# The rotated convolution of images 0 to 2 on 32x32 tiles of the array

## The reference

```python
x = x + L0(gn(x))   # deformable convolution: 36 points a pixel, 4 corners each, then two dense layers
x = x + L1(gn(x))   # rotated convolution, the layer that is changed
x = x + L2(gn(x))   # linear attention
x = x + L3(gn(x))   # three quantised depthwise-like convolutions
```

## Time and profile before

| | |
|---|---|
| Time, median of 3 runs (lowest, highest) | 8428.0 us (8407.72, 8446.78) |
| Profiled execution: its own time, its span | 8406.53 us, 8404.7 us |
| Mean granted clock of TensorE | 0.711 of full speed |
| Busy: TensorE, its weight loads | 3952.7 us (47%), 2022.5 us (24%) |
| Busy: VectorE | 5151.7 us (61%) |
| Busy: GpSimd (the gathers' instructions) | 4440.0 us (53%) |
| Busy: ScalarE | 1232.6 us (15%) |

### The profile page before, as it was taken

How to read it: one execution, slowest core, us unless ns; L and a number is a source line. 1 busy time by engine, 2 the same in 40 slices (tenths; PEclk the granted TensorE clock), 3 DMA queues, 4 the chain that set the end, 5 groups by cost and what they waited for, 6 DMA issues and landing times.

```text
span 8404.7 us, 44163 instructions
## 1 busy us (share of the span) xinstructions
PE 3952.7 (47%) x11246; PEld 2022.5 (24%) x11246; DVE 5151.7 (61%) x4233; ACT 1232.6 (15%) x1846; POOL 4440.0 (53%) x4684
## 2 busy tenths in 40 slices
PE   6133241341365535442555435442565544428797
PEld 3121121221122213221222113221222222213453
DVE  6667668576566646664666646654666665553556
ACT  1000100001111001111111001111110011112246
POOL 2666656666565655565665655565666555650000
PEclk8566665675687657766787667766787777669899
DMA  4442533534333322244333322244333223441128
GB/s 130 129 128 87 158 113 123 151 109 136 111 107 96 99 85 87 90 153 161 115 96 102 99 81 91 88 159 150 116 113 95 76 89 96 151 149 42 43 99 236
DMA packets 511085, 953.74 MB, mean 113 GB/s; under 512 B 252032, under 2 KB 300928, under 8 KB 494848
## 3 DMA queue, kind: packets, MB, share of 16 engines
q0 software_dynamic: 221184, 604.27, 23.3%
q1 hardware_dynamic: 289792, 348.19, 12.9%
HBM read 791.89 MB, written 160.24 MB: 113 GB/s over the span
## 4 chain that ended last, share of the span: by engine, by line
issue 30%; another core or an unknown queue 26%; DVE 17%; PE 17%; ACT 4%; POOL 3%; DMA 2%; DVEq 1%; SPq 1%; ACTq 0%; POOLq 0%
PE PS L859 16%; DVE ring L1700 6%; DVE dbuf L1706 3%; ACT img L1310 3%; POOL ring L482 3%; DVE PS L1882 1%; DMA img<-d_dram 1%; DVE cb L1767 1%; DVEq L384 1%; DVE img L2067 1%; ACT cb L1310 0%; DVE stats L1762 0%; DVE img L2183 0%; PE PS L1176 0%
## 5 line engine op out<-in xcount | busy, mean ns | idle before, releaser
L482 POOL DMA_INDIRECT ring<-table,idx_stage x4608 | 4422.2, 960 | 3021.7 <-DVE dbuf L1706 1550.4
L1706 DVE TENSOR_REDUCE dbuf<-ring 128x64 f32<-128x2304 f32 x512 | 2071.1, 4045 | 109.6 <-issue 79.8
L859 PE MATMUL PS<-img,wb_sb 128*128 128x512 f32 (+1 forms) x3264 | 1646.0, 665 | 989.4 <-issue 401.9
L1700 DVE TENSOR_TENSOR ring<-ring,PS 128x2304 f32<-128x2304 f32 x480 | 1222.6, 2547 | 119.6 <-DMA ring<-table,idx_stage 101.4
L859 PE MATMUL PS<-img,wa_sb 128*128 (+2 forms) x2908 | 944.3, 635 | 624.2 <-issue 459.7
L859 PEld LDWEIGHTS PS<-img,wb_sb 128*128 128x128 f32 x3264 | 688.3, 215 | 1913.2 <-issue 1692.9
L859 PEld LDWEIGHTS PS<-img,wa_sb 128*128 128x128 f32 (+2 forms) x2908 | 385.2, 166 | 1153.7 <-issue 1123.1
L859 PE MATMUL PS<-wb_sb,img 128*128 128x512 f32 x512 | 344.1, 837 | 518.3 <-ACT cb L1310 221.5
L859 PE MATMUL PS<-wa_sb,cb 128*128 128x256 f32 (+1 forms) x992 | 262.2, 427 | 542.4 <-issue 269.8
L2067 DVE SCALAR_TENSOR_TENSOR img<-PS,params,img 128x512 f32<-128x512 f32 x256 | 179.9, 744 | 507.2 <-ACT img L1310 358.9
L2230 DVE TENSOR_REDUCE sm<-PS 128x16 f32<-128x1024 f32 x64 | 78.3, 1224 | 610.3 <-remote 465.1
(11 more groups left out here) (253 smaller groups left out, 3305.4 us busy)
## 6 DMA issues: line engine op xcount, KB each, us to landing
ring<-table,idx_stage POOLq DMA_INDIRECT x4608
table<-cb SPq DMA_DIRECT2D x64, 512.0 KB
img<-y_dram SPq DMA_DIRECT2D x64, 512.0 KB
q_dram<-img SPq DMA_DIRECT2D x32, 1024.0 KB
img<-q_dram SPq DMA_DIRECT2D x28, 1024.0 KB
img<-in_x SPq DMA_DIRECT2D x8, 2048.0 KB
y_dram<-cb SPq DMA_DIRECT2D x64, 256.0 KB
img<-in_x SPq DMA_DIRECT2D x32, 512.0 KB
```

Of the source, the lines that this page charges most:

```text
L482: nc.gpsimd.indirect_dma_start(out=ring[:, g, p * CORNERS * GC:(p + 1) * CORNERS * GC], out_offset=None, in_=tab[b], in_offset=bass.Indire ...
L859: return nc.tensor.matmul(o, l, r, start=start, stop=stop, **kw)
L1700: last = vec.tensor_tensor(rg, rg, weights.unsqueeze(2).to_broadcast([P, n, GC]), ALU.mult)
L1706: vec.tensor_reduce(dbuf[:, j, g * GC:(g + 1) * GC], ring[:, g, :].rearrange("p (k c) -> p c k", c=GC), AX_X, ALU.add).then_inc(sem("ring_ ...
```

## The change

Images 0 to 2 now go through `l1_packed` too. They can't have bank 7, so they use banks 0 to 3 (`l1_bank`), and each group of four chunks waits until the group before it has been added. On VectorE a turn of the stage is one (quad, k): half of the turn's units, the wait, eleven additions, four statistics, the other half of the units. `lt` has one layout, copied in one instruction, and isn't cleared.

```diff
-        def packed(n):
-            return START + (B - 1) * CHUNKS + n
+        def packed(b, n):
+            return START + b * PAIRS + n
+        def l1_bank(b, j, k):
+            return 2 * j + k if b == B - 1 else j
@@ TensorE, L1
-                def l1(i):
-                    for h in range(2):
-                        n, c = i * 2 + (b * CHUNKS + h), i * 2 + h
-                        room(pe, "lX", n)
-                        for k in range(KC):
-                            for tap in range(K2):
-                                at = R_SIZE + (k * K2 + tap) * P
-                                last = mm(PS[:, 2 * h + k, :].rearrange("p (r x) -> p r x", x=W), wseg(wa_sb, at, P),
-                                          padded(k, c, tap // 3, tap % 3), tap == 0, tap == K2 - 1)
-                        last.then_inc(sem("lC"), 1)
                 def l1_packed(quad, k):
-                    if quad:
-                        pe.wait_ge(sem("lX"), packed(k + 1))
+                    if b < B - 1:
+                        pe.wait_ge(sem("lX"), packed(b, quad * KC + k))
+                    elif quad:
+                        pe.wait_ge(sem("lX"), packed(b, k + 1))
                     for tap in range(K2):
                         for j in range(4):
                             for r in range(4):
                                 ...
-                                last = mm(rows(PS[os_, 2 * j + k, :]), wa_sb[rs, at:at + CG],
+                                last = mm(rows(PS[os_, l1_bank(b, j, k), :]), wa_sb[rs, at:at + CG],
                                           padded(k, quad * 4 + j, tap // 3, tap % 3)[rs], tap == 0, tap == K2 - 1,
                                           tile_position=(r * CG, to * CG), skip_group_check=True)
-                if b < B - 1:
-                    loop(l1)
-                else:
-                    for quad in range(2):
-                        for k in range(KC):
-                            l1_packed(quad, k)
+                for quad in range(2):
+                    for k in range(KC):
+                        l1_packed(quad, k)
@@ VectorE, L1
-                if b == 0:
-                    link(vec.memset(lt, 0.0))
-                    lt4 = lt.rearrange("p (k t o) -> p k t o", k=KC, t=K2)
-                    for q in range(P // CG):
-                        r_ = slice(q * CG, (q + 1) * CG)
-                        last = vec.tensor_copy(lt4[r_, :, :, r_], sums[r_])
+                link(vec.tensor_copy(lt.rearrange("p (k n) -> p k n", k=KC), PS[:, 2:4, 0:K2 * CG]))
-                def l1(i):
-                    for h in range(2):
-                        n, c = i * 2 + (b * CHUNKS + h), i * 2 + h
-                        stream.give(1, 4)
-                        done(dve, "lC", n)
-                        for k in range(KC):
-                            last = vec.scalar_tensor_tensor(out=chunk_of(img1, k, c), in0=PS[:, 2 * h + k, :], ...)
-                        last.then_inc(sem("lX"), 1)
-                        done(dve, "lX", n)
-                        for k in range(KC):
-                            vec.bn_stats(seg(stats, c * 6 + k * 48, 6), chunk_of(img1, k, c))
-                        stream.give(1, 4)
-                if b < B - 1:
-                    chunks("L1" if gi != B - 1 else "L1 last", gi, 0, l1)
-                else:
-                    for quad in range(2):
-                        for k in range(KC):
-                            l1_packed(quad, k)
+                part = "L1" if gi != B - 1 else "L1 last"
+                if gi is not None:
+                    weights_for(gi)
+                for n in range(PAIRS):
+                    stream.begin(part, gi, n)
+                    stream.give(1, 2)
+                    l1_packed(n // KC, n % KC)
+                    stream.finish()
+                stream.ended(part, gi)
```

More of the change, by code:

```diff
@@ L2107, in L1 @@
                 link(vec.reciprocal(mod, mod))
-                lt = wseg(wa_sb, R_SIZE, KC * K2 * P)
-                if b == 0:
-                    link(vec.memset(lt, 0.0))
+                lt = wseg(wa_sb, R_SIZE, KC * K2 * CG)
                 if gi is not None and gi > 1:
@@ L2148, in L1 @@
                 dve.wait_ge(sem("l1_products"), (b + 1) * (K2 + 2))
-                sums = PS[:, 2:4, 0:K2 * CG].rearrange("p k (t o) -> p k t o", t=K2)
-                if b == B - 1:
-                    last = vec.tensor_copy(lt[:, 0:KC * K2 * CG].rearrange("p (k n) -> p k n", k=KC), PS[:, 2:4, 0:K2 * CG])
-                else:
-                    lt4 = lt.rearrange("p (k t o) -> p k t o", k=KC, t=K2)
-                    for q in range(P // CG):
-                        r_ = slice(q * CG, (q + 1) * CG)
-                        last = vec.tensor_copy(lt4[r_, :, :, r_], sums[r_])
-                link(last)
-                barrier()
-                def l1(i):
-                    for h in range(2):
-                        n, c = i * 2 + (b * CHUNKS + h), i * 2 + h
-                        stream.give(1, 4)
-                        done(dve, "lC", n)
-                        for k in range(KC):
-                            last = vec.scalar_tensor_tensor(out=chunk_of(img1, k, c), in0=PS[:, 2 * h + k, :], scalar=mod[:, k:k + 1],
-                                                            in1=chunk_of(img1, k, c), op0=ALU.mult, op1=ALU.add)
-                        last.then_inc(sem("lX"), 1)
-                        done(dve, "lX", n)
-                        for k in range(KC):
-                            vec.bn_stats(seg(stats, c * 6 + k * 48, 6), chunk_of(img1, k, c))
-                        stream.give(1, 4)
+                link(vec.tensor_copy(lt.rearrange("p (k n) -> p k n", k=KC), PS[:, 2:4, 0:K2 * CG]))
+                barrier()
                 def l1_packed(quad, k):
                     n = quad * KC + k
-                    dve.wait_ge(sem("lC"), packed(n + 1))
+                    dve.wait_ge(sem("lC"), packed(b, n + 1))
                     for j in range(4):
@@ L2182, in l1_packed @@
                             at = (first + j * CG) % P
-                            last = vec.scalar_tensor_tensor(out=img[to], in0=PS[at:at + width, 2 * j + k, :],
+                            last = vec.scalar_tensor_tensor(out=img[to], in0=PS[at:at + width, l1_bank(b, j, k), :],
                                                             scalar=mod[to, k:k + 1], in1=img[to], op0=ALU.mult, op1=ALU.add)
                     last.then_inc(sem("lX"), 1)
-                    dve.wait_ge(sem("lX"), packed(n + 1))
+                    dve.wait_ge(sem("lX"), packed(b, n + 1))
                     for j in range(4):
                         vec.bn_stats(seg(stats, (quad * 4 + j) * 6 + k * 48, 6), chunk_of(img1, k, quad * 4 + j))
-                if b < B - 1:
-                    chunks("L1" if gi != B - 1 else "L1 last", gi, 0, l1)
-                else:
-                    for quad in range(2):
-                        for k in range(KC):
-                            l1_packed(quad, k)
+                part = "L1" if gi != B - 1 else "L1 last"
[7 more added lines that the diff above has]
+                stream.ended(part, gi)
                 barrier()
```

## The result

The changed kernel takes 8534.7 us (median of 4 runs, 8516.28 to 8564.95) against 8418.9 for the kernel before (4 runs beside it, 8407.72 to 8446.78): ratio 1.0139, 95% interval [1.0104, 1.0175], slower. The profiled execution took 8531.26, its span 8529.5, which is 124.8 us more than the span before.

What follows compares the result with a forecast made beforehand. GpSimd's gathers were taken to bound the L1 stages, with small matmuls stuck beside them: +44, +44, +29 and -7 for setup make +110 on 8406.5, so 8517; adding half of 21 gave 8530 us, range 8390 to 8640.

Steps and rivals of the forecast that it cites:

- The bound (gathers, 335 us): L1 stage, image 0: GpSimd's gathers set a floor of 335 us; the stage took 375, the rest gaps in the gathers.
- rival 1: L1 stages: price goes by pass through the array, or none for small tiles; gaps vanish, -137 us, 8270; chance 0.13.
- 2.8 us a record, whatever its size: TensorE beside gathers: each record costs 2.8 us, not by columns or bytes; bounds for small ones 0.03 and 2.8 us.
- A store of about 54 records: TensorE: some 54 records pass once gathers run, then one per 2.8 us; a group has 288.
- Which groups are stuck: L1 stages: groups beginning beside gathers (1 and 3) can't end until these stop; alternative, 0 and 2 stuck, +58 us.
- The stages: L1 stages of images 0 to 2: +44, +44 and +29 us against 375, 375 and 207.4.
- The clock at the stage's start: TensorE at 1.2 GHz for the first 3 to 4 us, so some 265 records fit before gathers resume.
- Setup, -7: Ahead of the L1 stages: four copies of 0.75 us become one, -2.3 us an image, -7 in all.
- The rest keeps its length: Later stages (L2, A, F) should keep their lengths; moving beyond noise would mean something outside the prediction's steps is at work.
- Rival 2: L1 stages: small tiles go free but VectorE becomes late, 22 us an image on the path; -71 us, 8335; chance 0.04.
- Rival 3: L1 stages: all groups stuck, each waiting out a refill of the ring; +201 us, 8608; chance 0.12.
- rival 4: L1 stages: small records cost about a quarter, only group 3 stays late; no change to be told, 8410; chance 0.09.

Runs made afterwards that it cites:

- the traffic kernel: Changed kernel with one-megabyte loads from ScalarE's queue into an unused buffer in the L1 stages of images 0 to 2: 8507.7 us, one run, against 8441.3.
- the 256-column one: Kernel before, each 512-column convolution matmul of images 0 to 2 cut into two: 8519.2 us against 8441.3, ratio 1.0094; in another set 6806.6 us, 1.0003.
- the three-deep kernel: Kernel before with three chunks of PSUM instead of two in the convolution of images 0 to 2, loop written out: 6805.8 and 6806.1 us, ratios 1.0002 and 0.9997.

## Why the prediction was right, point by point

*The bound (gathers, 335 us)*: right, seen bare in the other condition: 333 and 347 us, and 168 in image 2 against 157 forecast by rival 1.

*2.8 us a record, whatever its size*: right for this condition. The small records of the changed kernel stand 2.8 us apart, which is the upper of the two bounds and the value taken, and half the columns in the unpacked kernel changed nothing. What it missed is that the price is one of 1.40 us for each instruction: between two records a weight load stands just as far from both,

```profile
2772.41 0.12 PEld L863 LDWEIGHTS PS<-img,wa_sb 32*32 32x32 f32 x1 [2.68 <-issue]
```

1.40 us after the record at 2771.01 and 1.40 before the one at 2773.81, which is also the distance of VectorE's products. A record pays for itself and for its weight load.

*A store of about 54 records*: mis-sized for the small ones. A fresh group passes 41 at once and then waits (2761.29 and 2974.81, and again 41 in image 1; in image 2 the 41 are followed by 104 more, in a pause of the gathers). It makes no difference to a group of 288.

*Which groups are stuck*: right for image 0 (1 and 3). Image 1 took the other pattern that the prediction had (0 and 2), 408.9 us against its 401. Image 2 took neither: groups 1 and 2 were late, with three pauses of 7, 30 and 25 us, so its 227 for the forecast 236 is no support for the steps.

*The stages*: forecast 419, 419 and 236 (+117 over before), measured 435, 409 and 227 (+113). Errors of opposite sign cancel, and so does the rest of the sum: 110 us were forecast for the profiled execution and 125 came, while the median before fell from 8428.0 to 8418.9. That 8530 lies within 5 us of 8534.7 is luck; that the time rises by some 1.4% is not.

In image 0 it is one term: after the gathers stop, the prediction let the records wait 12 us and then take 6. The rows say 2869.1 to 2884.5 and then 10.1, 7.5 more, and at the second stop 3093.3 to 3114.0 and 9.4, another 8 more than the 16 and 6 of the forecast: 16 us in all, which is 435 for 419. Half of it was a misreading of the kernel before. The prediction took 14 us for the wait after a long run of gathers, from their stop at 2993.7 to the addition at 3007.7, but there the records were still slow:

```profile
3013.13 1.01 PE L859 MATMUL PS<-img,wa_sb 128*128 x1 [3.20 <-issue]
3015.22 19.19 PE L859 MATMUL PS<-img,wa_sb 128*128 x39 [1.08 <-issue]
```

The slow spell ended 21.5 us after the stop, which is what the change shows (20.7). The other half is the clock, next.

*The clock at the stage's start*: I assumed 1.2 GHz for 3 to 4 us from the earlier trace rows. In image 0 it is granted in full there, in image 1 it is not; and it is at the lower level (0.50) where group 2 starts and where the 202 records run after the slow spell (windows of the stage's start, group 2's start, the first 5.04 us of the 202 records, their last 5.07, and the start of image 1's stage):

```profile
2726.20:2728.20 2.00, 1.98 (x66) 1.03 (x68) 1.91 (x2) 0.00 (x0) 0.00 (x0) 1.00 0.00 0
2903.04:2906.00 2.96, 2.96 (x59) 1.21 (x65) 2.93 (x6) 0.00 (x0) 0.00 (x0) 0.50 0.00 0
2884.46:2889.50 5.04, 5.04 (x67) 1.66 (x67) 0.00 (x0) 0.00 (x0) 0.00 (x0) 0.50 0.00 0
2889.50:2894.57 5.07, 5.07 (x151) 3.20 (x134) 0.00 (x0) 0.00 (x0) 0.00 (x0) 0.98 0.02 3
4648.00:4651.00 3.00, 3.00 (x64) 1.20 (x65) 2.93 (x3) 0.00 (x0) 0.00 (x0) 0.51 0.02 5
```

So the assumption held for group 2, and was missing where it cost time: the 202 records take 10 us because the clock is 0.50 for half of them, where I had taken image 3's 30.8 per us. Group 0 has the same 8.0 us ahead of the gathers in both images. At the full clock it ends; in image 1, at 0.51 for 3 us, it has passed 252 of its 288 records after 13.4 us and is caught. That the clock alone decides between the two patterns isn't shown, since VectorE's products had the 1.40 us price just before image 1's stage. One sum of the prediction is off by its own terms, without effect: 280 and 54 less the 3 to 4 us at the lower clock is 272 to 288, not 265.

*GpSimd's idleness*: forecast "from 42 to 80 us and more"; 44.3 + 48.6 = 93 us. VectorE's waits ahead of its additions were said to be 30 to 50 us; they are 62 and 67 in image 0. The prediction's own steps give about 50 for the first; 7.5 and 8 us of the excess are the later restart above.

*Setup, -7*: the stretches ahead of the three stages moved by +1, -19 and +5 us, -13 in all. The copies are too small to be told in this.

*The rest keeps its length*: it grew by about 24 us (124.8 - 113.1 + 12.6), which I had not forecast. I don't put it down to the change. VectorE's statistics of one stage to those of the next but one span 745 us before and 723 after in image 0, though the code between is the same; the traffic kernel has 733 and the 256-column one 749 for it. (In the changed kernel the two stand at 3161.34 and 3884.09.) The next stretch, up to the statistics ahead of image 1's L1 stage, is 28 us longer after the change than before, and 11 us longer in the traffic kernel, which runs the same code there. Differences of 10 to 30 us a stretch thus occur between these executions without a change in the code. By the prediction's own sign something outside its steps is at work there; the runs don't show what.

*The rivals*: rival 1 (no price for small tiles) is excluded in the 8400 condition by the rows at 2771 to 2777, yet in the 6800 condition its premise holds. Its gain doesn't come even there, because the large matmuls have no price either and are hidden as well: in the three-deep kernel (1.0002 and 0.9997 of the kernel before) TensorE's 134 us fit beside 332 us of gathers. Rival 2 (VectorE late) was seen nowhere. Rival 3 (all stuck) came true in no image; rival 4 (small records at a quarter of the price) falls with the rows too.

What the prediction did not see is that the 2.8 us belongs to a condition, and not to the kernel. It read the price off one trace and had no view that could tell.

## What to carry to other kernels

Before trading few large instructions for many small ones, look at what an instruction costs in the stretch where they will run, and not where the engine runs alone: here 864 packed records ran in 28 us where nothing was gathered, and 288 were held up for 133 us beside gathers. Where a ring of buffers couples two engines, a wait of the one costs what the engine that feeds the ring pauses for, and not the whole wait (here 44 us of 62, since four slots were filled meanwhile); so look for the pauses of the feeding engine. And if a stage is already as long as its gathers, a faster engine beside them gives nothing: compute that floor first.

## What the runs showed of the hardware that was not expected

The same program on the same chip (7) took 6804 us (31 runs, 6801 to 6809) and, in a later set, 8441 us (7 runs, 8424 to 8460). In the slower condition single instructions get a price beside gathers on two engines: 2.80 us on TensorE for 108, 256 and 512 columns, and on VectorE 1.40 us from one product of taps to the next. With the weight load between two records counted, both are 1.40 us an instruction. In the faster one VectorE's products of image 1, beside gathers 1.25 to 1.48 us apart, run without a break, 18 in 6.76 us, 0.38 each:

```profile
3650.12 6.76 DVE L2134 TENSOR_TENSOR cb<-wa_sb,cb 128x288 f32<-128x288 f32 x18
```

The gathers' busy time is the same in both (4415.3 and 4433.3 us), and so is their pace where they run (1.25 us each). What switches the condition was not found. Each timed run carries the profiler's span and clock, so it stays open whether writing the profiler's own records has a part in the price; a cost by instruction, after a burst that passes free, would fit it, but no run here left the recording out.

The Trainium skill (NOTIFIC — the notification-queue block, section 7.1) says that the block that writes such records holds its producers back, engines among them, when its internal pipeline is full, rather than lose a record. No run here shows whether that happened.

For whoever chooses between the two kernels: the change costs 1.4% in one condition, gains nothing that can be told in the other (0.9996 and 1.0001), and no version tried here beats the kernel before.
